# Attention values with the tokens on the partitions: split f16 probabilities stationary, V and a column of ones streamed, output turned back by 32-bit transposes

## The reference

```python
w1 = softmax(q1 @ k1.T)                      # 16 heads of 32, keys and values shared by pairs of heads
w2 = softmax(q2 @ k2.T)
attn = (w1 - lam * w2) @ v                   # 154 keys
rms = rsqrt(mean(attn * attn, axis=-1) + 1e-5)
attn = attn * rms * g * (1.0 - LAMBDA_INIT)
x = x + attn @ Wo.T
```

## Time and profile before

| | |
|---|---|
| median of three runs | 2326.67 us (2326.14 to 2328.17) |
| span of the profiled execution | 2319.4 us (7.3 us below the median of the runs) |
| TensorE busy | 2235.6 us, 96% |
| VectorE busy | 1713.3 us, 74% |
| ScalarE busy | 1396.2 us, 60% |
| GpSimd busy | 1075.1 us, 46% |
| granted TensorE clock, mean | 0.987 |

### The profile page before, as it was taken

One profiled execution on the slowest core, in us unless ns is written; L12 is line 12 of the kernel. 1 busy time (PEld: TensorE's weight loads), 2 busy tenths in 40 slices (PEclk: granted clock), 3 DMA queues, 4 the chain that ended last, 5 costly groups with the idle time before them and its releaser, 6 DMA issues.

```text
span 2319.4 us, 34978 instructions
## 1 busy us (share of the span) xinstructions
PE 2235.6 (96%) x13375; PEld 1049.7 (45%) x13375; DVE 1713.3 (74%) x2607; ACT 1396.2 (60%) x2037; POOL 1075.1 (46%) x851
## 2 busy tenths in 40 slices
PE   8679999999999999999999999999999999999977
PEld 5334435354453534445353444535344453534433
DVE  3768769586786958678695877869587786958673
ACT  3566557665565766566575656657655666755554
POOL 2403717255281725528172552817255281735417
PEclk9879999999999999999999999999999999999999
DMA  8313122031312203121220312122041212202000
GB/s 315 100 46 89 27 69 56 25 91 30 96 36 73 56 25 88 33 77 41 79 63 25 87 34 78 38 72 57 25 103 33 76 41 70 59 25 69 16 23 19
DMA packets 172291, 142.64 MB, mean 62 GB/s; under 512 B 91688, under 2 KB 140396, under 8 KB 171612
## 3 DMA queue, kind: packets, MB, share of 16 engines
q1 hardware_dynamic: 169116, 135.23, 22.5%
q0 software_dynamic: 3008, 5.18, 0.7%
HBM read 51.80 MB, written 20.36 MB: 31 GB/s over the span
## 4 chain that ended last, share of the span: by engine, by line
PE 79%; DVE 10%; issue 3%; SPq 3%; ACT 2%; DMA 2%; POOL 1%; POOLq 0%; ACTq 0%; DVEq 0%
PE ps L1540 19%; PE ps L1562 10%; PE ps L1382 7%; PE ps L1552 6%; PE ps L1434 6%; PE ps L1383 6%; PE ps L1384 6%; PE ps L1485 5%; PE ps L1461 5%; PE ps L1492 4%; DVE attn_raw L1112 3%; SPq L492 2%; PE ps L1466 2%; PE ps L1573 1%; PE ps L1530 1%
## 5 line engine op out<-in xcount | busy, mean ns | idle before, releaser
L643 POOL TENSOR_TENSOR attn_raw<-attn_raw 128x512 f32<-128x512 f32 x448 | 642.2, 1452 | 51.6 <-ACT attn_raw L813 23.2
L1540 PE MATMUL ps<-rows,w1T 128*128 128x512 f16 x2048 | 483.6, 379 | 6.1 <-DVE rows L1168 6.1
L609 POOL TENSOR_TENSOR q<-q 128x512 f16<-128x512 f32 x128 | 150.0, 1176 | 617.6 <-ACT q L757 616.3
L1074 DVE TENSOR_REDUCE arena<-ps 128x3 f32<-128x462 f32 (+1 forms) x704 | 403.3, 612 | 33.4 <-PE ps L1434 31.6
L1173 DVE SCALAR_TENSOR_TENSOR arena<-attn_raw,vec_cols,arena 128x512 f16<-128x512 f32 x256 | 278.8, 1089 | 60.6 <-ACT arena L811 56.9
L808 ACT ACTIVATE attn_raw<-ps,vec_cols,wstep 128x512 f32<-128x512 f32 x256 | 198.3, 775 | 171.0 <-PE ps L1540 168.0
L1540 PEld LDWEIGHTS ps<-rows,w1T 128*128 128x128 f16 x2048 | 191.4, 97 | 197.4 <-DVE rows L1168 9.5
L777 ACT ACTIVATE arena<-ps 128x1024 f32<-128x1024 f32 x128 | 131.4, 1027 | 235.4 <-PE ps L1461 235.4
L1562 PE MATMUL ps<-w2T,arena 128*128 128x512 f16 x1088 | 271.1, 378 | 0.0
L1094 DVE SCALAR_TENSOR_TENSOR p<-arena,p 128x512 f16<-128x512 f32 x128 | 88.1, 688 | 241.6 <-ACT p L781 241.6
L1434 PE MATMUL ps<-k_att,stack_raw 96*128 96x154 f16 x2048 | 217.7, 232 | 10.8 <-DVE arena L1074 8.2
(11 more groups left out here) (181 smaller groups left out, 3397.7 us busy)
## 6 DMA issues: line engine op xcount, KB each, us to landing
stack_raw<-q SPq DMA_DIRECT2D x744, 64.0 KB, 2.0
arena<-in_x SPq DMA_DIRECT2D x64, 256.0 KB, 2.7
out<-arena SPq DMA_DIRECT2D x64, 256.0 KB, 2.0
arena<-in_x SPq DMA_DIRECT2D x14, 1024.0 KB, 6.3
arena<-in_L_ffn_w SPq DMA_DIRECT2D x7, 1024.0 KB, 16.8
rows<-in_x SPq DMA_DIRECT2D x2, 1024.0 KB, 7.3
stack_raw<-in_L_xattn_Wq SPq DMA_DIRECT2D x8, 256.0 KB, 11.1
k_att<-k_store SPq DMA_DIRECT2D x4, 490.0 KB
```

The source lines that it names most:

```text
L643: ins = pool.tensor_tensor(acc[:, e, :], acc[:, e, :], src[:, j % NG, :], ALU.add)
L1074: dve.tensor_reduce(negmax[:, tt, u0:u1], ps[:, row_bank(c, tb), 0:(u1 - u0) * S].rearrange("p (u s) -> p u s", s=S), AX.X, ALU.max, negat ...
L1540: ins = pe.matmul(ps[:, B_H + j % 2, :], w1T[:, k, j * P:(j + 1) * P], rows16[:, e, k, :], start=(k == 0 and e == 0), stop=(k == KD - 1 an ...
```

## The change

The probabilities of all keys are split into f16 high and low parts, and become the stationary side of the value product, 128 tokens at a time. V (also split) is the moving side; each of its high parts has a 33rd column of ones, so that the product gives 32 channels and the sum of the probabilities beside them, tokens on the partitions. Per head group and 128 tokens there are 3 matmuls for the rest keys (132, 132 and 128 columns) and 12 for the main keys (33, 33 and 32 columns): 60 per group, each with its own 128x128 f16 weight load. The sums are divided out in that layout on VectorE (a reciprocal of 16 columns, a product with it), the second softmax is subtracted after the odd group, and the quarter is turned back by four 32-bit 128x128 transposes on TensorE (`transpose_attn`) into the bank `B_SREST`, which is the one that the rest scores use. The mean square is taken from batch-norm statistics on VectorE; the squares on ScalarE, their sums on GpSimd, `rms_sums` and the copies of the even group are gone.

New work per head group: two ScalarE copies f32 to f16 of 128x1024, one VectorE copy of 128x512, one VectorE subtraction of 128x1536 and one GpSimd subtraction of 128x1024. The constant 1024 by which the probabilities are scaled comes from a third added row of the score product, so `STKM` is 99. `scores` of group 5 waits for the split of quarter 0, that of group 7 for quarter 1, since the bank is shared. Values are loaded per batch by four DMAs instead of one, two of them with pieces of 32 f16. The token strings are changed (`t` in the place of `a`).

```diff
 ATTEND = [(w[0], int(w[1:] or 0)) for w in (
-    "e2 g f2 y0 y1 s0 q0 z0 z1 y2 s1 v0 s2 h3 v1 s3 i3 v2 y3 s4 a0 v3 s5 q1 z2 v4 s6 a1 q2 v5 z3 s7 q3 v6 a2 v7 a3").split()]
+    "e2 g f2 y0 y1 y2 s0 q0 z0 z1 z2 s1 h3 v0 s2 i3 v1 y3 z3 s3 q1 v2 s4 q2 t0 v3 s5 q3 v4 s6 t1 v5 s7 v6 t2 v7").split()]
+SCORES_BEFORE = {0: 5, 1: 7, 2: QM, 3: QM}
...
-FIRST = tokens("r1 w0 s0 b0 w1 s1 x1 w2 v0 w3 q0 s2 w4 v1 w5 s3 w6 v2 q1 w7 s4 a0 v3 w8 w9 s5 q2 v4 w10 s6 a1 v5 q3 w11 s7 v6 w12 "
-               "a2 v7 w13 a3 w14 w15")
+FIRST = tokens("r1 w0 s0 b0 w1 s1 x1 w2 v0 w3 s2 q0 w4 v1 w5 s3 w6 v2 w7 s4 q1 t0 w8 v3 w9 s5 q2 w10 v4 s6 t1 w11 v5 s7 q3 w12 v6 t2 "
+               "w13 v7 w14 w15")
...
+        v_att = sb("v_att", [P, KV * (VC + DH) + MR * (VC + DH)], F16)
+        v_main = v_att[:, 0:KV * VC].rearrange("p (h c) -> p h c", c=VC)
+        v_main_lo = v_att[:, KV * VC:KV * (VC + DH)].rearrange("p (h c) -> p h c", c=DH)
+        v_rest = v_att[:, KV * (VC + DH):KV * (VC + DH) + MR * VC].rearrange("p (m i c) -> p m i c", i=UPT, c=VC)
+        v_rest_lo = v_att[:, KV * (VC + DH) + MR * VC:].rearrange("p (m i c) -> p m i c", i=UPT, c=DH)
...
-        o_first, l_first, cross_a, cross_b, l_prod = (attn_raw[:, n * TB:(n + 1) * TB] for n in range(4, 9))
+        o_norm = [attn_raw[:, n * TB:(n + 1) * TB] for n in range(2)]
+        attn = attn_raw[:, 2 * TB:3 * TB].rearrange("p (t d) -> p t d", t=TT)
...
+                hi, lo, rest_hi, rest_lo = (v_store[b][:, n0:n1] for n0, n1 in (
+                    (0, VM), (VM, 2 * VM), (2 * VM, 2 * VM + MR * DH), (2 * VM + MR * DH, 2 * VM + 2 * MR * DH)))
+                sp.dma_start(v_main[:, :, 0:DH], hi.rearrange("p (h d) -> p h d", d=DH)).then_inc(s_vatt, 16)
+                sp.dma_start(v_main_lo, lo.rearrange("p (h d) -> p h d", d=DH)).then_inc(s_vatt, 16)
+                sp.dma_start(v_rest.rearrange("p m i c -> p (m i) c")[:, :, 0:DH],
+                             rest_hi.rearrange("p (h d) -> p h d", d=DH)).then_inc(s_vatt, 16)
+                sp.dma_start(v_rest_lo.rearrange("p m i d -> p (m i d)"), rest_lo).then_inc(s_vatt, 16)
...
+            def probs_lo(c, gi):
+
+                wait(pool, s_p_hi, c, 2 * QM, 2 * gi + 1)
+                split = p_split[gi % 2]
+                pool.tensor_tensor(split[:, 1, 0:2, :], probs[:, gi % 2, 0:2, :], split[:, 0, 0:2, :],
+                                   ALU.subtract).then_inc(s_lo_pool, 1)
...
                     elif what == "q" and ahead:
                         q_lo(i + 1, n)
...
                 act.activation(probs[:, buf, 0:2, :], ps[:, 0:2, :], ACT.Exp).then_inc(s_p, 1)
                 wait(act, s_s, c, 2 * QM, 2 * gi + 2)
                 act.activation(probs[:, buf, 2:5, :], ps[:, 2:5, :], ACT.Exp).then_inc(s_p, 1)
-                wait(act, s_p, c, 2 * QM, 2 * gi + 2)
-                act.mul(p16[:, buf, 0, :], probs[:, buf, 4, :], PSCALE).then_inc(s_r_hi, 1)
+                for half in range(2):
+                    wait(act, s_p, c, 2 * QM, 2 * gi + half + 1)
+                    act.copy(split[:, 0, 2 * half:2 * half + 2, :],
+                             probs[:, buf, 2 * half:2 * half + 2, :]).then_inc(s_p_hi, 1)
...
             def attn_hi(c, mp):
-                wait(act, s_att, c, KD, mp + 1)
+                wait(act, s_attT, c, KD, mp + 1)
                 if c == 0 and mp == 0:
                     act.wait_ge(s_xt, 2 * TT)
-                act.mul(attn16[:, 0, mp, :], attn[:, mp % 2, :], ASCALE / OSCALE).then_inc(s_att_hi, 1)
-                if mp == 1:
-                    wait(act, s_rms, c, 1, 0)
-                elif mp >= 2:
-                    wait(act, s_sqsum, c, KD - 1, mp - 1)
-                act.activation(attn_sq[:, mp % 2, :], attn[:, mp % 2, :], ACT.Square,
-                               scale=1.0 / OSCALE).then_inc(s_sq, 1)
+                act.copy(attn16[:, 0, mp, :], ps[:, B_SREST, :]).then_inc(s_att_hi, 1)
...
-            def rest_lo(c, gi):
+            def probs_lo(c, gi):
+                buf, split = gi % 2, p_split[gi % 2]
+                wait(dve, s_p, c, 2 * QM, 2 * gi + 2)
+                dve.tensor_copy(split[:, 0, 4, :], probs[:, buf, 4, :]).then_inc(s_r_hi, 1)
+                wait(dve, s_p_hi, c, 2 * QM, 2 * gi + 2)
                 wait(dve, s_r_hi, c, QM, gi + 1)
-                dve.scalar_tensor_tensor(p16[:, gi % 2, 1, :], probs[:, gi % 2, 4, :], PSCALE, p16[:, gi % 2, 0, :],
-                                         ALU.mult, ALU.subtract).then_inc(s_r_lo, 1)
+                dve.tensor_tensor(split[:, 1, 2:5, :], probs[:, buf, 2:5, :], split[:, 0, 2:5, :],
+                                  ALU.subtract).then_inc(s_lo_dve, 1)
 
             def normalise(c, gi):
 
-
-                mp = gi // 2
-                if gi % 2 == 0:
-                    return
-                b_o, b_l = value_banks(gi)
-                wait(dve, s_ol1, c, KD, mp + 1)
+                mp, odd = divmod(gi, 2)
+                sums = ps[:, B_O:B_L + 1, 0:2 * UPT * VC].rearrange("p b (u c) -> p b u c", c=VC)
                 wait(dve, s_pv, c, QM, gi + 1)
+                dve.reciprocal(l_inv[:, odd, :, :], sums[:, :, :, DH]).then_inc(s_inv, 1)
+                wait(dve, s_inv, c, QM, gi + 1)
                 wait(dve, s_att, c, KD, mp)
-                dve.tensor_tensor(cross_b, ps[:, b_o, :], l_first, ALU.mult).then_inc(s_o2, 1)
-                dve.tensor_tensor(cross_a, ps[:, b_l, :], o_first, ALU.mult)
-                dve.tensor_tensor(l_prod, ps[:, b_l, :], l_first, ALU.mult).then_inc(s_ol2, 1)
-                wait(dve, s_ol2, c, KD, mp + 1)
-                dve.scalar_tensor_tensor(cross_a, cross_b, neglam[:, 0:1], cross_a, ALU.mult, ALU.add).then_inc(s_diff, 1)
-                dve.reciprocal(l_prod, l_prod).then_inc(s_inv, 1)
-                wait(dve, s_inv, c, KD, mp + 1)
-                if mp >= 2:
-                    wait(dve, s_sq, c, KD, mp - 1)
-                dve.tensor_tensor(attn[:, mp % 2, :], cross_a, l_prod, ALU.mult).then_inc(s_att, 1)
+                dve.tensor_tensor(o_norm[odd].rearrange("p (b u d) -> p b u d", b=2, d=DH), sums[:, :, :, 0:DH],
+                                  l_inv[:, odd, :, :].unsqueeze(3).broadcast_to([P, 2, 2 * UPT, DH]),
+                                  ALU.mult).then_inc(s_norm, 1)
+                if odd:
+                    wait(dve, s_norm, c, QM, gi + 1)
+                    wait(dve, s_attT, c, KD, mp)
+                    dve.scalar_tensor_tensor(attn.rearrange("p t d -> p (t d)"), o_norm[1], neglam[:, 0:1], o_norm[0],
+                                             ALU.mult, ALU.add).then_inc(s_att, 1)
+                    wait(dve, s_att, c, KD, mp + 1)
+                    for tt in range(TT):
+                        ins = dve.bn_stats(attn_stats[:, tt, mp, :], attn[:, tt, :])
+                    ins.then_inc(s_ast, 1)
 
             def attn_lo(c, mp):
                 wait(dve, s_att_hi, c, KD, mp + 1)
-                dve.scalar_tensor_tensor(attn16[:, 1, mp, :], attn[:, mp % 2, :], ASCALE / OSCALE, attn16[:, 0, mp, :],
-                                         ALU.mult, ALU.subtract).then_inc(s_att_lo, 1)
+                dve.tensor_tensor(attn16[:, 1, mp, :], ps[:, B_SREST, :], attn16[:, 0, mp, :],
+                                  ALU.subtract).then_inc(s_att_lo, 1)
+
+            def rms_variance(c):
+
+                wait(dve, s_ast, c, KD, KD)
+                dve.memset(gate[:], 0.0)
+                for tt in range(TT):
+                    ins = dve.bn_aggr(attn_mv[:, tt, :], attn_stats[:, tt, :, :].rearrange("p m s -> p (m s)"))
+                ins.then_inc(s_aag, 1)
+                wait(dve, s_aag, c, 1, 1)
+                dve.tensor_tensor(attn_meansq, attn_mv[:, :, 0], attn_mv[:, :, 0], ALU.mult).then_inc(s_amq, 1)
+                wait(dve, s_amq, c, 1, 1)
+                dve.scalar_tensor_tensor(var[:, 1, :], attn_meansq, EPS * VSCALE * VSCALE, attn_mv[:, :, 1], ALU.add,
+                                         ALU.add).then_inc(s_var2, 1)
...
-                    wait(pe, s_ol1, c - 1, KD, KD)
+                    wait(pe, s_norm, c - 1, QM, QM)
...
                     wait(pe, s_p, c, 2 * QM, 2 * gi)
+                    wait(pe, s_att_lo, c, KD, sum(n <= gi for n in SCORES_BEFORE.values()))
...
             def values(c, gi):
 
-                m, buf = ORDER[gi] % (QM // 2), gi % 2
-                b_o, b_l = value_banks(gi)
-                wait(pe, s_p, c, 2 * QM, 2 * gi + 2)
+                mp, split = ORDER[gi] % (QM // 2), p_split[gi % 2]
+                wait(pe, s_lo_dve, c, QM, gi + 1)
+                wait(pe, s_lo_pool, c, QM, gi + 1)
+                wait(pe, s_norm, c, QM, gi)
                 if gi == 0:
-                    pe.wait_ge(s_vatt, 16 * (c // BLK_PER_BATCH + 1))
+                    pe.wait_ge(s_vatt, 64 * (c // BLK_PER_BATCH + 1))
                     if c == 0:
                         wait(pe, s_xt_lo, 1, TT, TT)
-                elif gi % 2 and gi < QM - 1:
```

(61 more changed lines are left out.)

## The result

The changed kernel takes 2518.95 us, median of 4 runs (2513.29 to 2523.23), against 2326.4 us (2325.69 to 2328.17) for the kernel before on the same chip: ratio 1.0827, 95% interval 1.0809 to 1.0845, 8.3% slower. The forecast was 2484, the range 2395 to 2545. Medians and ratios are of undisturbed runs; one run of experiment 6, at 4142.57 us, is left out of its ratio.

The account below looks back on a forecast made before the run. TensorE's own work set the time before; afterwards it would wait for the chain through ScalarE, GpSimd and VectorE. Span 2319.4 + 149 (16 blocks at 9.3) + 9 for loads = 2477, plus 7 around it: 2484 us, range 2395 to 2545.

Parts of the forecast that it names:

- TensorE's own work: Value product 2.95 to 1.98 us a group; with added transposes and dropped sums of squares, a block some 7 us shorter.
- The rival of 56 ns: Value product: a matmul of 33 columns costs as much as one of 128, 7 us per block, 2596 us; chance 0.03.
- the 81 ns: Skill page's price per load and matmul at 128 columns; value product 4.9 us a group, 2716 us in all.
- The chain: Exponentials, copies, GpSimd's then VectorE's subtraction behind a group's scores: low parts done at s + 8.2; net 9.3 us per block.
- the wait for `y3`: Before q1, between scores 3 and 4, TensorE idles 3.5 us for VectorE's addition, queued behind group 2's subtraction.
- Segment by segment: TensorE's stretches between score starts, then v7, to the projection: 62.0 us a block against 51.8, 10.2 more.
- The loads: Three value loads in the loop, ahead of query stacking on SyncE's queue, 3 us each: 9 us with longer fills at start.
- The 7 us around the span: Time outside the profiled span, taken to stay 7 us as before, making 2477 into 2484 us.
- The forecast case: TensorE waits for the longer chain, VectorE held up by GpSimd, no clock fall: 2484 us; chance 0.40.
- the rival with the clock: TensorE's clock falls in the 5.5 us gap before v7, costing 1.7 us per block: 2511 us; chance 0.24.
- VectorE is not held up: VectorE's subtraction runs beside GpSimd's, low parts at s + 6.85, 4.1 us per block: 2402 us; chance 0.17.
- The other engines keep up: TensorE's work alone decides, -7.1 us per block: 2222 us; chance 0.09.

Follow-up runs that it names:

- experiment 6: Changed kernel without the split from block 1 on: exponentials write f16 directly, copies, cast and both subtractions left out, same number of matmuls; 2326.83 us, ratio 1.0012.
- experiment 12: Kernel of experiment 6 with y3 ahead of v1, transposes in the queries' bank, and low-part matmuls of the probabilities left out from block 1 on; 2191.87 us, ratio 0.9434.
- experiment 2: Changed kernel with GpSimd's subtraction cut to 4 of 512 columns from block 1 on, same number of matmuls; 2448.59 us, ratio 1.0531.
- experiment 8: Changed kernel with VectorE subtracting all 128x2560 itself from block 1 on, GpSimd doing none; 2518.79 us, ratio 1.0837.
- experiment 10: Changed kernel with products two groups behind scores, transposes in the queries' bank, VectorE's normalisation moved forward, and its cast moved to ScalarE; 2422.43 us, ratio 1.0411.
- experiment 1: Changed kernel with VectorE's addition y3 moved ahead of the normalisation of group 1, nothing left out; 2502.15 us, ratio 1.0758.
- Experiment 4: Kernel of experiment 1 plus 36 unread matmuls of 512 columns a block in TensorE's gaps, blocks 1 to 14; 2474.94 us, ratio 1.0647.
- experiment 3: Kernel of experiment 2 with VectorE's subtraction cut to 4 columns as well, same number of matmuls; 2395.5 us, ratio 1.0314.

## Why the prediction was right, and where its terms were off

**TensorE's own work.** 2.95 to 1.98 us was forecast for a value product, 1.90 measured at full clock; matmuls of 33 columns stand 25 to 26 ns apart, where 27 was taken from the row with 2 columns. The rival of 56 ns is out, by the trace and by experiment 12, and so are the 81 ns of the Trainium skill's page "TensorE: Matmul & The Clock Gate", section "Back-to-back issue gap": at full clock no load and matmul of 128 columns took that long in a row, and 56 ns holds in both traces. In the changed kernel this saving bought nothing, as TensorE's work no longer set the time.

**The chain.** Forecast were low parts at s + 8.2; those of group 4 ended 7.75 us after its scores. GpSimd began 0.15 us earlier and took 0.15 less than forecast, and what VectorE had left behind it took 1.61 instead of 1.75. VectorE's subtraction was put at 1.75 us free and some 3 when held up: 1.76 and 2.85 measured. Experiments 2 and 8 show that the hold-up is real. In 8 the two engines do no better than VectorE alone, which is what turns would give and what a shared bandwidth that favours neither would not have to. VectorE's 2.85 us end 1.61 us after GpSimd's instruction, close to the 1.76 it needs free, so it did nearly nothing before; in experiment 10, where it starts 0.4 us later, it again ends 1.61 us after GpSimd (901.07 against 899.46). The cast, with one input, was held as well: 2.27 us in experiment 1. That was not in the prediction, and it helped the number by luck: the low parts of group 2, on which the wait for `y3` was built, were done at s + 8.3, near the 8.2 forecast, but by a held cast of 1.46 us and a late start, with a free subtraction of 1.76. The Trainium skill, page "SBUF — State Buffer", section "Who interferes with whom", has both, the instruction with two SBUF inputs and a cast in its fast mode, as instructions that exclude GpSimd; the rows agree. That the cast ran in such a mode is not shown, only that its 512 columns took 0.43 us by themselves, where a subtraction of 512 took 0.69.

**Segment by segment,** forecast and measured, us: scores 0 to 1 3.9 and 3.9; to 2 6.8 and 6.65; to 3 6.8 and 7.1; to 4 9.35 and 11.8; to 5 9.0 and 8.5; to 6 5.9 and 7.4; to 7 9.0 and 8.5; to `v7` 9.3 and 8.8; `v7` 2.0 and 2.7; sum 62.0 and 65.3. Where the chain binds, the forecast is a little high, by 0.5 us each. The three that are too low, by 2.4, 1.5 and 0.7 us, are the ones with a query product or `v7` behind a gap: `q1` took 5.07 instead of 2.60 us, scores 5 and `q3` together 5.5 instead of 3.9, `v7` 2.7 instead of 1.9. The idle time before `q1` was forecast to 0.3 us (3.5, measured 3.2). The projection took 10.85 us (10.9 forecast).

**The term that was mis-sized is the clock.** The forecast left it at nothing, and its rival let it fall once a block, before `v7`, for 1.7 us. It rested on the one long gap of the trace before, where the clock held for 4 us of idleness. But that gap stood behind other work than these; here the clock falls around gaps of 1.7 to 3.8 us, five times in most blocks and three times in blocks 11 to 13. Those three blocks give its price without any change of the kernel: two falls more cost 64.1 - 61.0 = 3.1 us, and 4.3 where the one at `q1` lasts longer, as in the middle block. Over the eleven blocks that have them this is 8 x 3.1 + 3 x 4.3 = 38 us. Experiment 4 agrees, with at least 1.9 us a block. In the middle block the three long segments are 4.6 us above the forecast, the shorter ones give 1.7 back, and with 0.3 between scores 2 and 3 that is a net 3.2.

**The chain was priced too high, and that hid a part of the clock's price.** In blocks 12 and 13, with three falls left, a block grew by 143.5 - 135.1 = 8.4 us, and 0.8 of that is `v7` at the lower clock; the forecast had 9.3 with no fall at all. So 2484 is as near as it is by two errors of opposite sign.

**The loads.** The forecast had three loads at 3 us each, since queries would wait behind them on SyncE's queue, and that is what happens. In a block before a new batch the stretch from the projection to the next scores is 6.1 to 6.5 us longer than in the others, where it was 1.1 to 2.0 longer before: 4.5 to 5.0 each, 14 us together, a fall of the clock there included. SyncE takes 5.9 us to issue the four loads, where the one took 0.9. The last of the four in SyncE's timeline, then ScalarE, which waits until the stacking has read its buffer (in block 4 the same instruction waits for TensorE):

```profile
662.94 3.11 SPq L482 DMA_DIRECT2D v_att<-v_store  x1
```

```profile
675.45 0.60 ACT L778 ACTIVATE q<-ps 128x512 f32<-128x512 f32 x1 [9.20 <-DMA stack_raw<-q]
```

No run loads the values otherwise, so what a better load would give back is not shown.

**Sum.** Scores of block 0 began 4.8 us later (141.3 instead of 136.5), and from there to the end of the span 191.6 us were added: 16 x 8.4 = 134 for the blocks, 38 for the clock's further falls, 14 for the loads, and 5 that are mostly block 0's. Forecast were 149, nothing, 9 with the start, and nothing: 158, where 196.4 were measured. The 7 us around the span were wrong as well: the profiled execution after took 2517.57 us for a span of 2515.8, so 1.8 lie around it, as in the runs of the kernel before (2329.88 us for a span of 2328.1). By that the profiled execution before took some 2321 us, 5 less than the median. The forecast case was the right one, and the rival with the clock, 2511, had the nearer number, with a mechanism of the right kind; its place and price were not. At `v7` the clock costs 0.8 us and not 1.7, and the larger part fell at `q1`, scores 5 and `q3`, so that its total is near by luck.

**The other rivals.** "VectorE is not held up" would have given 2402, and experiment 2, which takes the hold-up away with GpSimd's instruction, gave 2449 with the clock still at 0.935: 70 us less against the 82 of the forecast. "The other engines keep up", 2222, was further off than its working shows: even with no split at all (experiment 6) the same order of work took 2327, since `q1`'s wait for `y3` and the gaps at the transposes remain, and only with the order mended 2251.

**Not foreseen** was how waits for one busy engine replace each other: 36 us taken from `q1` gave 17, 61 taken from the scores gave 41.

## What to carry to other kernels

Before work is moved from the engine that bounds to others that look idle, write down when the first consumer needs the result: 1.0 us a group saved on TensorE was paid with a chain of 7.75 us from scores to the last operand where it had been some 4.3 (3.02 + 0.63 + 0.69), though ScalarE and VectorE had 40% and 26% to spare. A step that frees a buffer belongs ahead of long work on the same engine: one engine's order was worth 207 us between two kernels with the same instructions. And ask of a second engine that shares a step whether it adds anything: GpSimd's 266 us here added nothing.

## What the runs showed of the hardware

- TensorE's granted clock fell to 0.50 around gaps of 1.7 to 3.8 us that followed each other at 5 to 16 us, though it had held 1.00 for 4 us of idleness in the earlier trace rows. The same gap of 3.2 us before `q1` brought it down in eleven of the blocks 1 to 14 and not in the other three; what decides it is open. With the gaps partly filled by matmuls of 512 columns it was low for at most 5.4 us of the stretch from scores 0 to the projection, where it was low for 13.3 to 20.2 us in the same blocks without them (experiments 4 and 1).
- At the lower clock matmuls of 33 columns still started 28 to 29 ns apart (25 to 26 at full clock), but a value product took 2.7 us instead of 1.9, since those of 132 columns went from 57 to 110 ns or so, and a query product 5.07 instead of 2.60.
- While GpSimd ran its subtraction of 1024 columns, VectorE's subtraction of 1536 and its cast made nearly no headway: 2.85 us instead of 1.76, and up to 2.27 instead of 0.43. VectorE alone does all 2560 columns in 2.82 us (experiment 8).
- From these, (2.82 - 1.76) / 1024 = 1.04 ns a column on VectorE, so 0.17 us fixed, where 0.15 was estimated; in experiment 3 a subtraction cut to 12 columns took 0.17 us.
- Four bn_stats of 128 columns took 0.87 us, and the reciprocal of 16 columns 0.25 us, where 0.1 was forecast.
